# Bias tiles made by VectorE, a shorter matmul lag, and all stores begun on SyncE, in a two-stage mixing kernel

## The reference

```python
# x is (1, 16, 1024, 1024): 16 heads, 1024 rows (queries), 1024 columns (keys)
rel = jnp.tril(idx[:, None] - idx[None, :])                   # distance, 0 above the diagonal
pos = jnp.maximum(rel.max(axis=-1), threshold)[:, None]       # one number for each row
nd = jnp.log(jnp.abs(c * rel) + 1.0) / (jnp.log(jnp.abs(c * pos) + 1.0) + EPS)
h = jax.nn.relu(nd[..., None] * W1[0] + b1)                   # 32 hidden values for each (row, column)
x = x + (jnp.einsum('qkm,mh->qkh', h, W2) + b2).transpose(2, 0, 1)[None]
# then, for each (t, s), a 16x16 mix of the heads:
ret = x @ (w + eye)                                           # shared
ret += rank-2 term and diagonal from qw1, qw2, qdd            # depends on the row t
ret += rank-2 term and diagonal from kw1, kw2, kdd            # depends on the column s
```

## Time and profile before

| what | value |
|---|---|
| median of 3 runs | 1018.52 us (1011.3 to 1022.31) |
| the profiled execution | 1017.06 us, its span 1015.1 us |
| busy: TensorE, ScalarE, VectorE, GpSimd | 755.0, 453.8, 373.5, 344.3 us |
| mean granted TensorE clock | 0.89 of full |
| DMA | 149.50 MB, 147 GB/s over the span |
| loads on SyncE's queue, stores on ScalarE's | 39.3% and 27.6% of the 16 engines' span |

### The profile page before, as it was taken

The page is one execution under the profiler, slowest core; times in us unless marked ns, Lnnn a source line. Parts: engine busy times, 40 slices in busy tenths (PEclk is TensorE's granted clock), DMA queues, the critical chain, the costliest instruction groups (busy, mean ns, idle before and its releaser), DMA issues.

```text
span 1015.1 us, 37021 instructions
## 1 busy us (share of the span) xinstructions
PE 755.0 (74%) x17186; PEld 545.3 (54%) x17186; DVE 373.5 (37%) x358; ACT 453.8 (45%) x472; POOL 344.3 (34%) x189
## 2 busy tenths in 40 slices
PE   2269697688767796697965978777796687867973
PEld 1029654486536753485534955347553485534963
DVE  7970265205640274204541045310354103541041
ACT  6554264444553263443653435534264443653400
POOL 7461044202440053202863027630276402771000
PEclk9679988798979997789999989979899798996997
DMA  6974799844997178943899138892388923790079
GB/s 112 204 163 82 191 201 238 191 103 107 226 205 175 41 164 214 200 107 85 179 203 201 47 85 183 206 191 49 83 154 211 200 67 79 168 214 3 5 161 194
DMA packets 366437, 149.50 MB, mean 147 GB/s; under 512 B 99660, under 2 KB 366028, under 8 KB 366284
## 3 DMA queue, kind: packets, MB, share of 16 engines
q1 hardware_dynamic: 229068, 80.02, 39.3%
q10 hardware_dynamic: 137216, 67.13, 27.6%
HBM read 77.61 MB, written 69.47 MB: 145 GB/s over the span
## 4 chain that ended last, share of the span: by engine, by line
PE 42%; SPq 15%; ACTq 15%; ACT 9%; issue 8%; DMA 4%; POOL 3%; DVE 3%; POOLq 0%; DVEq 0%
PE main L609 22%; ACTq L196 15%; PE main L599 11%; PE bias L622 9%; SPq L223 9%; ACT hidden L376 4%; SPq L230 4%; POOL hidden L339 3%; ACT hidden L371 3%; DMA mats_a<-a_mats 3%; ACT y L385 2%; DVE mixed L510 1%; DMA a_mats<-mixed 1%; DMA b_mats<-mixed 1%; DVE y L523 1%
## 5 line engine op out<-in xcount | busy, mean ns | idle before, releaser
L339 POOL TENSOR_TENSOR hidden<-log_table,row_scale 128x1024 f32<-128x1024 f32 x176 | 340.1, 1950 | 573.4 <-PE bias L622 560.7
L376 ACT ACTIVATE hidden<-hidden,b_col 128x1024 f32<-128x1024 f32 x176 | 197.6, 1144 | 293.6 <-issue 153.5
L622 PE MATMUL bias<-hidden,w_blocks 128*64 128x512 f32 x768 | 229.9, 714 | 129.2 <-ACT hidden L376 84.3
L510 DVE TENSOR_TENSOR mixed<-main,mixed 128x1024 f32<-128x1024 f32 x128 | 156.7, 1224 | 440.0 <-PE main L599 440.0
L599 PEld LDWEIGHTS main<-y,mats_a 32*32 32x32 f32 x8192 | 241.9, 131 | 121.2 <-issue 58.4
L599 PE MATMUL main<-y,mats_a 32*32 32x128 f32 x8192 | 271.3, 280 | 42.1 <-DMA mats_a<-a_mats 28.0
L609 PE MATMUL main<-y,mats_b 32*32 32x128 f32 x8192 | 258.0, 281 | 51.1 <-issue 37.8
L609 PEld LDWEIGHTS main<-y,mats_b 32*32 32x32 f32 x8192 | 243.3, 132 | 74.4 <-issue 46.5
L398 ACT ACTIVATE mixed<-main 128x1024 f32<-128x1024 f32 x128 | 130.9, 1023 | 199.5 <-PE main L609 194.2
L622 PEld LDWEIGHTS bias<-hidden,w_blocks 128*64 128x64 f32 x768 | 54.8, 155 | 233.5 <-issue 189.3
L523 DVE SCALAR_TENSOR_TENSOR y<-bias,b_col,x_stage 128x1024 f32<-128x1024 f32 x64 | 82.2, 1284 | 142.7 <-PE bias L622 142.7
(11 more groups left out here) (37 smaller groups left out, 27.5 us busy)
## 6 DMA issues: line engine op xcount, KB each, us to landing
x_stage<-in_x SPq DMA_DIRECT2D x512, 128.0 KB, 5.3
out_mixed<-mixed ACTq DMA_DIRECT2D x256, 128.0 KB, 4.4
out_mixed<-mixed ACTq DMA_DIRECT2D x128, 256.0 KB
mats_a<-a_mats SPq DMA_DIRECT2D x256, 32.0 KB
b_mats<-mixed SPq DMA_DIRECT2D x2, 512.0 KB, 6.1
mats_b<-b_mats SPq DMA_DIRECT2D x8, 128.0 KB, 2.8
a_mats<-mixed SPq DMA_DIRECT2D x2, 512.0 KB, 9.5
mixed<-in_L_conv_kw SPq DMA_DIRECT2D x2, 128.0 KB, 2.6
```

What stands on the lines that cost most here:

```text
L339: nc.gpsimd.tensor_tensor(hidden_tile(h).rearrange("p (j s) -> p j s", j=ROWS), bass.AP(logs.tensor, logs.offset, [list(logs.ap[0]), [1, R ...
L376: nc.scalar.activation(hidden_tile(h), hidden_tile(h), ACT.Relu, bias=b1_col[:, 0:1])\
L510: dve.tensor_tensor(at, main[:, T % 2, :].rearrange("p (t s) -> p t s", t=ROWS), at, ALU.add).then_inc(main_taken, 1)
L622: mm = pe.matmul(bias[into, T % 2, at:at + BANK], w2_blocks[:, g, :], hidden_tile(hidden_index(k, T, g))[:, at:at + BANK], start=True, sto ...
```

## The change

- LAG goes from 4 to 2: row tile s is followed by bias tile s - 2.
- In two-group regions the second group's hidden tile of every odd T is made by VectorE (`by_dve`), in 8 TENSOR_SCALAR instructions of one row (multiply by the row's scale, maximum with -b1). relu(v + b1) is max(v, -b1) + b1; the missing W2.b1 goes into a third column of `b2_col`. ScalarE makes no tile alone any more. GpSimd makes 24 of 32 hidden tiles of such a region (28 before), VectorE 8.
- SyncE begins all stores, piece by piece, once the piece's last row tile is in `mixed`.
- x chunks 6 and 7 of each next region are begun by ScalarE in steps 4 to 7 of the row phase, four DMAs a step; chunks 0 to 5 of the region after stay on SyncE, behind the last stores.
- ScalarE makes the first hidden tiles of the next region in steps 0 and 1 of the row phase.
- Setup: the row part of `compact` moves to GpSimd, in five instructions after hidden tiles 1, 3, 5, 7 and 9; its transposes come before bias tile 12 (6 before); `take_turned` moves to ScalarE; x chunks 6 and 7 of region 0 are loaded ahead of the wait for the column matrices.

```diff
-LAG = 4
+LAG = 2
-SPREAD = (2, 4, 4, 2, 2, 1)
-        def row_by_row(k, T, g):
-            return groups_of(k) == 2 and g == 1 and T % 4 == 3
+        def by_dve(k, T, g):
+            return groups_of(k) == 2 and g == 1 and T % 2 == 1
 # SyncE, within the steps of a row phase
+                    for i in range(PIECES):
+                        if T == piece_end(i):
+                            sp.wait_ge(main_taken, a_tile(k, T) + 1)
+                            for b in range(BLOCKS):
+                                store_block(sp, k, i, b).then_inc(out_done[i], DMA)
                     if U is not None and U % XTILES == XTILES - 1:
                         q = x_index(k + 1, U) + XSLOTS
                         if q // XCHUNKS == k + 1 and q < REGIONS * XCHUNKS:
-                            load_x(q)
+                            continue
 # GpSimd, region 0, after the hidden tile of an odd T below 10
+                    if k == 0 and T % 2 == 1 and T < 10:
+                        compact_part(T // 2)
 # ScalarE, step s of a row phase
-                    for i, spread in enumerate(SPREAD):
-                        part = s - piece_end(i) - 1
-                        if 0 <= part < spread:
-                            if part == 0:
-                                act.wait_ge(main_taken, a_tile(k, s - 1) + 1)
-                            for b in range(BLOCKS // spread * part, BLOCKS // spread * (part + 1)):
-                                store_block(act, k, i, b).then_inc(out_done[i], DMA)
-                        U = s - LAG + 1
-                        if 0 <= U < TILES:
+                        U = s if s < 2 else s - LAG + 1
+                        if U < TILES and s != LAG:
                             make_hidden(k + 1, U)
+                    part = s - LAG - XTILES
+                    if 0 <= part < 2 * (XCHUNKS - XSLOTS) and k + 2 <= REGIONS:
+                        q = (k + 1) * XCHUNKS + XSLOTS + part // 2
+                        if part % 2 == 0:
+                            wait_x_slot(act, q)
+                        for b in range(BLOCKS // 2 * (part % 2), BLOCKS // 2 * (part % 2 + 1)):
+                            load_x_block(act, q, b)
 # VectorE
+            def make_hidden(k, T):
+                h = hidden_index(k, T, 1)
+                dve.wait_ge(hidden_used, h - RING + 1)
+                dve.wait_ge(scales_in, DMA)
+                t0 = k * W + T * ROWS
+                for j in range(ROWS):
+                    at, of_row = t0 - SLOTS * W + j, (t0 + j) % PART
+                    one = dve.tensor_scalar(hidden_tile(h)[:, j * W:(j + 1) * W], log_table[:, at:at + W],
+                                            row_scale[:, of_row:of_row + 1], neg_b1[:, 0:1], ALU.mult, ALU.max)
+                one.then_inc(dve_hidden_ready, 1)
 ...
                     if U is not None and k + 1 < REGIONS:
+                        if U + 1 < TILES and by_dve(k + 1, U + 1, 1):
+                            make_hidden(k + 1, U + 1)
                         add_bias(k + 1, U)
```

More of the change, by code:

```diff
@@ L268, in _ @@
             save_mats("b")
+            for q in range(XSLOTS, XCHUNKS):
+                load_x(q)
             sp.wait_ge(mats_out["b"], 2 * DMA)
@@ L271, in _ @@
             load_mats_b()
-            for q in range(XSLOTS, XCHUNKS):
-                load_x(q)
             save_mats("a")
@@ L502, in _ @@
             dve.wait_ge(const_bias_read, 1)
-            compact("b")
+            step(dve.tensor_copy(b2_col[:, 2:3], b2_col[:, 0:1]))
+            dve.tensor_tensor(b2_col[P // 2:, 2:3], b2_col[P // 2:, 0:1], bias[P // 2:, 1, 1:2], ALU.add)\
+               .then_inc(const_bias_read, 1)
+            step(dve.tensor_scalar(neg_b1[:], b1_col[:], -1.0, None, ALU.mult))
+            compact_columns()
+            dve.wait_ge(weights_in["a"], 4 * DMA)
+            eye = diagonal(w_eye, 1)
+            dve.tensor_scalar(eye, eye, 1.0, None, ALU.add).then_inc(eye_added, 1)
             def finish_tile(k, T):
@@ L563, in transposes @@
             def transposes(part):
[L564 removed]
+                pe.wait_ge(comp_made[part], 1)
                 if part == "a":
```

158 lines of the change are left out of this document (85 added, 73 removed).

## The result

The changed kernel takes **1102.22 us** (median of 4 runs, 1097.12 to 1107.69), the kernel before 1018.69 beside it: ratio 1.0831, 95% interval 1.0749 to 1.0913. The forecast was 1033 with a range up to 1075: the sign was right, the size wrong by 69 us. The profiled execution took 1104.29, its span 1102.1. A kernel's executions fall into a faster and a slower state, and the ratios compare fast ones alone while the medians take in all, so in experiments 1 to 4, where only one execution of the kernel before (996.07 us) was fast, the ratios lie above the quotient of the medians and their intervals are wide.

The account below looks back on a forecast made before the run. No engine was full; each region was a chain, TensorE setting the pace in steady two-group steps. Terms 3 + 6 - 4 - 7 + 14 + 2 + 2 = +16 on 1017.06 gave 1033 us, 8-in-10 range 965 to 1075.

Parts of the forecast that it names:

- Train (5.6 us): Two-group row phases: VectorE's eight instructions for a hidden tile alternate with two GpSimd tiles and take 5.6 us.
- loop (11.0): Two-group row phases: VectorE's eight instructions, bias tile, row tile and VectorE's take make two steps cost 11.0 us.
- rival 4: Two-group loop: TensorE's clock falls as it stands 3.3 of 11 us; +101, 1134 us, or 1067 partly; chance 16%.
- The rival's partial form: Two-group loops: TensorE's clock falls in only a third of them, giving 1067 us; within the clock rival's 16%.
- SyncE's stream: Row phases: SyncE issues all stores and row matrices, 62 us with contention; one-group third column tile waits until 72.5.
- Last region (+2): Last region: 48 stores and 16 matrices in one stream take 58 us against 56.3, +2.
- Setup (+3): Setup: GpSimd's 16 us of moved work delays storing the row matrices to 71 from 68.20, +3.
- region 0 (+6): Region 0: SyncE's stores begin only after matrix and x loads, until 133; +6 beyond the setup.
- Rival 1: Two-group phases: VectorE keeps the port, its eight instructions take 1.8 us; 942 us; chance 13%.
- Rival 2: Two-group phases: one GpSimd tile falls among VectorE's eight instructions, -61, 972 us; chance 15%.
- Rival 3: SyncE's stores: issuing them in one stream costs nothing, one-group stores land 14 us earlier; 993 us; chance 8%.
- What was to be seen: Changed profile: L586 mean near 0.7 us; ScalarE waits some 19 us for out_mixed in regions 1 to 3, none in 5 to 7.

Follow-up runs that it names:

- experiment 1: Changed kernel, but ScalarE makes the second group's odd hidden tiles in 8 activations, not VectorE: 1015.93 us, ratio 1.0132.
- experiment 2: Changed kernel, but ScalarE begins the stores again and SyncE x chunks 6 and 7: 1063.10 us, ratio 1.0614.
- experiment 3: Kernel before with VectorE's trains alone; LAG 4, stores and setup as before: 1063.34 us, ratio 1.0563.
- Experiment 4: Changed kernel, but in two-group phases TensorE computes each odd row tile from 3 on twice: 1043.32 us, ratio 1.0339.
- experiment 5: Changed kernel, but VectorE makes only 2 of 8 rows of its hidden tiles, the rest left out: 1018.85 us, one run.
- experiment 12: Changed kernel with odd tiles by ScalarE and stores split between SyncE and ScalarE, the last region's all on ScalarE: 963.67 us, ratio 0.9553.
- experiment 8: Kernel before with LAG = 2 as its only change: 982.20 us, ratio 0.9700.
- experiment 11: Changed kernel with LAG = 4, ScalarE's x loads moved to steps 6 to 9: 1087.43 us, ratio 1.0756.
- experiment 7: Changed kernel with odd tiles by ScalarE, which also begins store pieces 4 and 5, SyncE pieces 0 to 3: 969.43 us, ratio 0.9633.
- experiment 9: Changed kernel with its trains kept, but ScalarE begins store pieces 4 and 5: 1062.01 us, ratio 1.0478.

## Why the prediction was wrong

- **Train (5.6 us) and loop (11.0).** Right: 5.35, and 10.6 at full clock. The alternation by single instructions is shown by the source view and by experiment 5. The 20 us that the forecast gave the lag and the free ScalarE in one-group row phases came too (53.2 and 58.6 for 72.2 and 77.1).
- **"Against it: the two-group windows have TensorE busy 0.78" (rival 4, 16%).** This is the step that failed. That busy share was read from whole windows of the kernel before, whose row phases had no stand of 2.9 us in every loop; the forecast itself put 3.3 us of standing into each. The nearest row was in the earlier trace rows: 3.68 behind a stand of 6.36, twice as long as this one. The rival's partial form, a third of the loops, gave 1067 on its own, and the rest of the misses came on top. Experiment 4 shows it: with the stand filled the loop takes 10.6 us at clock 1.00, and the four row phases together 47 us less. Size: 33 of the 71 us that the windows miss, since the forecast's loop was longer than that of full clock.
- **SyncE's stream (62 us, estimate of 3 for contention).** The mechanism was right, the third column tile of windows 1 and 2 waits for it. Its size was not: 69.2 us, and 79.0 and 84.1 us to the third column tile, not 72.5. The mis-sized term is the price of an issue, 0.644 and 0.640, which are medians of the earlier trace rows. The maxima beside them are over 3 us, and a stream pays the mean: in the kernel before the recorded issues average 0.76 us for a store of 128 KB, 1.10 for one of 256 KB and 0.89 for the row matrices. The sum of 32, 16 and 32 issues at these is 70 us, an estimate from the trace of the kernel before alone. The 1.1 for 256 KB was right, and the 3 us for contention had no row behind them. Size: 6.5 and 11.6 of the 24.5 us in windows 1 and 2; the column tiles behind took another 6. These two windows were forecast shorter than before and came out longer, so for them the sign was wrong as well.
- **Last region (+2).** Mis-sized by the same prices: from 1042.47 to 1098.02 the 48 stores and 16 matrices took 55.6 us where the sum has 48.4. The sixteen stores of 256 KB took 1.15 each, the last sixteen of 128 KB 0.73, the first 32 issues 0.72 to 0.95. TensorE also waited for late row matrices there (2.70 and 1.52 us). Measured +8.7, undone by experiments 2 and 12.
- **Setup (+3) and region 0 (+6).** +5.5 and +9.5. GpSimd's four large moved instructions took 3.7 to 4.6 us each. Not tested apart, and one profile each does not settle the setup: the setup of the kernel before took 111.6 us, and next to unchanged 113.3 in experiment 3 and 116.8 in experiment 8.
- **LAG.** The forecast never priced it alone. It is a gain of 32 us (experiment 8) that the train's loop swallows: with trains the row phases are 101 us with a lag of 2, 106 in experiment 3 and 100 in experiment 11 with 4.
- **Rivals 1 to 3.** One and two are out: 31 of 32 trains hold two tiles. Rival 3 is out by experiments 7 and 9, where the same DMAs from two queues gave 46 and 40 us. The Trainium skill's rule (DMA: Bandwidth & Descriptors, "Issuing engines are not separate DMA queues") that spreading starts over engines only saves the time to initiate them, usually small relative to the DMA, does not say what many in a row cost. Here one start took 0.65 to 1.31 us, less than the 4.2 us (median) in which a store landed, but 80 of them in a row were on the path.
- **What was to be seen.** ScalarE waits for `out_mixed` in regions 1 to 3 and not later: seen, 82.5 us in 3, so 26 to 28 each where 19 was forecast. A mean of 0.7 us for L586: 0.733. Both held while the total did not: signs of a mechanism do not test what it costs.

## What to carry to other kernels

When a forecast creates a new regular stand on TensorE, price the work behind it at the lower clock too, and look for the clock in rows right behind such a stand, not in a window's average. Place a train of short VectorE instructions where GpSimd is idle (one step made 72 us here), and price a queue by the mean of its issues, not by the median, over its whole stream. Cut a bundled change into its parts before judging it: here a lag worth -32 us was hidden under a train of +48 and a queue of about +40. The parts do not simply add up: with the short lag the same train cost 86 us (experiment 1).

## What the runs showed that I had not expected

- More work was faster: with doubled row tiles the windows of the two-group phases were 41 us shorter in all, and the granted clock in region 4's phase 0.96 instead of 0.83.
- The clock did not fall behind every stand of 2.86 us: of 28 bias tiles behind one, two took 1.94 and 26 took 2.38 to 3.68. What decides it no run here shows; behind the 28 stands of 1.0 us in experiment 4, 27 took 1.94 and one 2.25, that one too at clock 1.00.
- A VectorE `tensor_scalar` stood for a whole GpSimd tile (1986 ns against 339), but `scalar_tensor_tensor` on PSUM ran in its 1.28 us beside one.
- Eight stores of 128 KB took 5.20 us to begin at the head of the stream and 6.48 in its middle, eight of 256 KB 9.83. Whether ScalarE's issues or the transfers under way raise it is open, but the kernel before has such issues as well.
